# A layer with two attentions and a ternary feed-forward: the last tile's transposed context read from memory, and the maximum scans of two weights moved

## The reference

```python
x = x + cross(layernorm(x), ctx_2048)          # x: 16 x 64 x 1024, ctx_2048: 16 x 1601 x 1024
x = x + diff_attention(layernorm(x))           # causal, 8 heads, within each batch of 64 tokens
x = x + ffn(layernorm(x))

def cross(x1, c):                              # 16 batches
    energy = einsum('bcn,bmn->bcm', x1, c)     # 64 x 1601, contraction over n = 1024
    attn = softmax(energy, -1)
    attn = attn / (1e-9 + attn.sum(axis=1, keepdims=True))
    x_r = einsum('bcm,bmn->bcn', attn, c)      # contraction over m = 1601
    t = x1 - (conv_w @ x_r + conv_b)
    return x1 + relu(batchnorm(t))             # statistics over all batches

def ffn(x):                                    # W1: 4096 x 1024, W2: 1024 x 4096
    h = gelu(x @ ternarize(W1).T + b1)
    return fake_quant_4bit(h @ ternarize(W2).T + b2)

def ternarize(W):                              # needs max |W| of the whole matrix first
    delta = 0.05 * max(abs(W)); mask = abs(W) > delta
    return sum(abs(W) * mask) / max(sum(mask), 1) * sign(W) * mask
```

## Time and profile before

| | |
|---|---|
| median of three runs | 1379.93 us (1379.62 to 1380.21) |
| the profiled execution | 1379.24 us, its span 1377.4 us |
| PE busy | 1334.1 us (97%) |
| DVE busy | 878.7 us (64%) |
| ACT busy | 495.1 us (36%) |
| moved by DMA | 356.25 MB, mean 259 GB/s |

### The profile page before, as it was taken

The page is one execution under the profiler, slowest core; times in us unless marked ns, Lnnn a source line. Parts: engine busy times, 40 slices in busy tenths (PEclk is TensorE's granted clock), DMA queues, the critical chain, the costliest instruction groups (busy, mean ns, idle before and its releaser), DMA issues.

```text
span 1377.4 us, 17833 instructions
## 1 busy us (share of the span) xinstructions
PE 1334.1 (97%) x6850; PEld 651.2 (47%) x6850; DVE 878.7 (64%) x1484; ACT 495.1 (36%) x765; POOL 2.4 (0%) x10
## 2 busy tenths in 40 slices
PE   7999999999999979999999999999999999999994
PEld 4554646444454434444555555444444444444442
DVE  3232424324242288888889996755999997777974
ACT  1121302113021122116877775112545455544432
POOL 0000000000000000000000000000000000000000
PEclk9999999999999989999999999999999999999998
DMA  9999999999999587845565669341487775222264
GB/s 379 419 421 420 421 422 420 422 421 421 417 398 393 234 321 255 315 168 164 161 182 154 172 174 339 107 168 52 167 271 226 242 264 196 77 77 77 77 180 152
DMA packets 141044, 356.25 MB, mean 259 GB/s; under 512 B 63008, under 2 KB 89760, under 8 KB 115360
## 3 DMA queue, kind: packets, MB, share of 16 engines
q1 hardware_dynamic: 137792, 343.56, 68.5%
q10 hardware_dynamic: 3168, 11.54, 2.1%
HBM read 308.40 MB, written 46.66 MB: 258 GB/s over the span
## 4 chain that ended last, share of the span: by engine, by line
PE 74%; issue 14%; DMA 6%; DVE 4%; ACT 1%; DVEq 0%; POOLq 0%; POOL 0%
PE ps L1048 13%; PE ps L1153 13%; PE ps L1309 9%; PE ps L1220 8%; PE ps L962 7%; PE ps L1269 6%; PE ps L1107 5%; PE ps L1000 4%; DMA ctxT<-in_ctxT 3%; PE ps L979 2%; PE ps L1030 2%; PE ps L982 2%; DMA w_scan<-in_w2t 1%; PE ps L1173 1%; DMA x_t<-in_x 1%
## 5 line engine op out<-in xcount | busy, mean ns | idle before, releaser
L1358 PE MATMUL ps<-t_half,hl 128*128 128x512 f16 x896 | 193.6, 379 | 0.0
L1048 PE MATMUL ps<-ctx_sb,attnT 128*64 128x512 f32 (+1 forms) x832 | 180.3, 593 | 0.0
L699 ACT ACTIVATE stg<-ps 128x512 f32<-128x512 f32 (+1 forms) x80 | 44.4, 555 | 345.5 <-PE ps L979 173.4
L1358 PEld LDWEIGHTS ps<-t_half,hl 128*128 128x128 f16 x896 | 87.7, 98 | 105.7
L962 PE MATMUL ps<-ctxT,x1T 128*64 128x512 f32 x512 | 115.8, 596 | 1.8 <-DMA ctxT<-in_ctxT 1.8
L872 ACT ACTIVATE hl<-hb,al 128x512 f16<-128x512 f32 x112 | 79.2, 720 | 97.4 <-PE ps L1358 83.7
L1048 PEld LDWEIGHTS ps<-ctx_sb,attnT 128*64 128x64 f32 (+1 forms) x832 | 58.9, 137 | 115.4 <-issue 108.0
L1862 DVE SCALAR_TENSOR_TENSOR hl<-hb,al,hl 128x512 f16<-128x512 f32 x112 | 81.9, 749 | 48.7 <-ACT hl L872 48.5
L1107 PE MATMUL ps<-wv_sb,x2T 128*128 128x512 f32 x256 | 112.0, 596 | 0.0
L1220 PE MATMUL ps<-wo_sb,oT 128*128 128x512 f32 x256 | 111.6, 593 | 0.3 <-ACT oT L778 0.3
L1456 DVE COPY stg<-ps 128x512 f32<-128x512 f32 (+1 forms) x80 | 50.9, 639 | 82.2 <-PE ps L982 43.0
(11 more groups left out here) (220 smaller groups left out, 1810.5 us busy)
## 6 DMA issues: line engine op xcount, KB each, us to landing
ctxT<-in_ctxT SPq DMA_DIRECT2D x64, 1024.0 KB, 22.4
ctx_sb<-in_ctx SPq DMA_DIRECT2D x40, 1024.0 KB, 17.3
ctx_sb<-in_ctx SPq DMA_DIRECT2D x8, 4096.0 KB, 28.3
ctx_sb<-in_ctx SPq DMA_DIRECT2D x16, 2048.0 KB, 32.5
w_scan<-in_w1t SPq DMA_DIRECT2D x32, 512.0 KB, 6.4
w_buf<-in_w1t SPq DMA_DIRECT2D x32, 512.0 KB, 4.1
w_scan<-in_w2t SPq DMA_DIRECT2D x32, 512.0 KB, 5.5
w_buf<-in_w2t SPq DMA_DIRECT2D x32, 512.0 KB, 4.7
```

The lines of the kernel that those rows point to most:

```text
L1048: ins = mm(bank(ea + hf)[C * b:C * b + C, :], attnT[0:w, slots[mt], C * b:C * b + C], ctx_sb[0:w, mt, b, hf * BANK:hf * BANK + BANK], star ...
L1358: ins = mm(bank(b), hl[:, r % RING, n, s * P:s * P + P], t_half[:, r % BRING, :], start=(fresh and k == 0 and n == 0), stop=(k == HK - 1 a ...
```

## The change

Tile 7 has no transposes. The host gives two more layouts of the context: `ctxW`, the rows 1024 to 1535 transposed, and `ctxE`, the last 65 rows of tile 7 transposed. SP loads tile 7's share: two pieces of `ctxW` into the ring, two into `stg`, and two of `ctxE` into `tail0` (where `x_t` lay) and `tail1` (where tile 6's `x1T` lay). PE multiplies from there (`loaded_energies`, `tail_energies`), and the copies of ACT and DVE go. Tile 7's `load_N` stand behind these loads and in the order in which the last tile uses them. `tok` and `xo` are loaded in two parts each, the second behind `wv`; on ACT `relu(2)` stands behind tile 0's copies. Of the scans, 32 (all of W1) stand in the value projection, spread between the parts of a tile's work by `V_SCANS`, and all 32 of W2 in the output projection: four ahead of `normal(H)`, five after each tile until they are done (tiles 0 to 4, and three after tile 5).

```diff
--- before.py
+++ after.py
 SINGLES = [(mt, half) for mt in range(TM, MT) for half in range(2)]
-PAIRS = [("wide", c) for c in range(NC)] + SINGLES[-2:]
-E = len(PAIRS)
-assert len(SINGLES) == E
+LOADED = (0,) * (NT - 2) + (0, NC)
+
+
+def pairs(p):
+
+    if p < BY_ROW:
+        return SINGLES
+    return [("wide", c) for c in range(LOADED[p], NC)] + (SINGLES[-2:] if p < NT - 1 else [])
+
+
+def first_pair(p):
+
+    return sum(len(pairs(q)) for q in range(p))
+
+
+def slots_of_tile(p):
+
+    ring = [(p, "chunk", c) for c in range(NC)] + [(p, "wide", i) for i in range(min(LOADED[p] // 2, 2))]
+    return ring if p < NT - 1 else ring + [(p, "apart", i) for i in range(2)]
+
+
+USES = [use for p in range(NT) for use in slots_of_tile(p)]
+USE_NO = {use: n for n, use in enumerate(USES)}
+RING_NO = {use: n for n, use in enumerate([use for use in USES if use[1] != "apart"])}
+RING_USES = list(RING_NO)
...
-SCANS_V = 48
+SCANS_V = 32
+V_SCANS = (0, 0, 2, 5, 6, 6, 6, 6, 1)
...
+        def slot(use):
+
+            return ctxT[:, RING_NO[use] % SLOTS, :, :] if use[1] != "apart" else stg[:, 2 * use[2]:2 * use[2] + 2, :, :]
+
+        def halves(use):
+
+            return slot(use) if use[1] == "apart" else slot(use).rearrange("p c (b m) -> p c b m", b=2)
...
-            def load_T(q, chunks):
+            def load_T(q, chunks, kind="chunk"):
                 for c in chunks:
-                    k = NC * q + c
+                    use = (q, kind, c)
+                    k = RING_NO[use]
                     if k >= SLOTS:
-                        sp.wait_ge(ctxT_used, k - SLOTS + 1)
-                    sp.dma_start(ctxT[:, k % SLOTS, :, :], ctxT_in[q, c]).then_inc(ctxT_got[k % SLOTS], 16)
+                        sp.wait_ge(ctxT_used, USE_NO[RING_USES[k - SLOTS]] + 1)
+                    to, src = (slot(use), ctxT_in[q, c]) if kind == "chunk" else (halves(use), ctxW_in[q, c])
+                    sp.dma_start(to, src).then_inc(ctxT_got[k % SLOTS], 16)
+
+            def load_apart():
+
+                sp.wait_ge(e_done, first_pair(NT - 1))
+                for i in range(2):
+                    sp.dma_start(slot((NT - 1, "apart", i)), ctxW_in[NT - 1, 2 + i]).then_inc(apart_got, 16)
+                for i in range(2):
+                    sp.dma_start(tails[i][:, :, :, :], ctxE_in[i]).then_inc(apart_got, 16)
...
                     load_T(p + 1, range(7, NC))
+                    load_T(p + 1, range(min(LOADED[p + 1] // 2, 2)), "wide")
+                    if p + 1 == NT - 1:
+                        load_apart()
+                        next_N((5, 7, 0, 1, 2, 6, 3, 4))
+                        break
                     next_N(range(0, 5))
...
-            sp.wait_ge(ctxT_used, NC * NT)
+            def load_tok(t0, t1):
+                sp.dma_start(tok[:, t0:t1, :], n_dram[t0:t1].rearrange("t p n -> p t n")).then_inc(n_in, 16)
+
+            def load_xo(t0, t1, s):
+                sp.dma_start(xo[:, t0:t1, :], x_v[t0:t1].rearrange("t p n -> p t n")).then_inc(s, 16)
+
+            sp.wait_ge(ctxT_used, len(USES))
             sp.wait_ge(n_stored, 16 * (NT - 1))
-            sp.dma_start(tok[:, 0:NT - 1, :], n_dram[0:NT - 1].rearrange("t p n -> p t n")).then_inc(n_in, 16)
+            load_tok(0, 2)
             sp.wait_ge(pv_done, G * NT - 7)
-            for i in range(2):
-                h4 = slice(4 * i, 4 * i + 4)
-                sp.dma_start(xo[:, h4, :], x_v[h4].rearrange("t p n -> p t n")).then_inc(s_in[i], 16)
+            load_xo(0, 2, s_in[0])
             sp.wait_ge(pv_done, G * NT - 3)
             sp.dma_start(wv_sb[:, :, :], wv.rearrange("(c p) n -> p c n", p=P)).then_inc(wv_in, 16)
+            load_tok(2, NT - 1)
+            load_xo(2, NT, s_in[1])
             sp.wait_ge(pv_done, G * NT)
...
-                if n == 34:
+                if n == 28:
                     sp.wait_ge(xs_ready, 6)
                     load_qk(0)
...
-                if t + 2 < NT:
+                if 1 <= t < NT - 2:
...
+                if t == 0:
+                    act.wait_ge(n_in, 32)
+                    relu(2)
...
+            def loaded_energies(p):
+
+                wides = [u for u in slots_of_tile(p) if u[1] != "chunk"]
+                for j, use in enumerate(wides):
+                    if use[1] == "apart":
+                        pe.wait_ge(apart_got, 64)
+                    else:
+                        k = RING_NO[use]
+                        pe.wait_ge(ctxT_got[k % SLOTS], 16 * (k // SLOTS) + 16)
+                    for i in range(2):
+                        c = 2 * j + i
+                        for b in range(2):
+                            ins = mm(bank(2)[C * b:C * b + C, :], x1T[:, p % 2, c, C * b:C * b + C], halves(use)[:, i, b, :],
+                                     start=(c == 0), stop=(c == NC - 1))
+                    ins.then_inc(ctxT_used, 1)
+
+            def tail_energies(p):
+                for c in range(NC):
+                    for b in range(2):
+                        ins = mm(bank(3, TAIL)[C * b:C * b + C, :], x1T[:, p % 2, c, C * b:C * b + C],
+                                 tails[c // 4][:, c % 4, b, :], start=(c == 0), stop=(c == NC - 1))
+                ins.then_inc(e_done, 1)
...
                 weigh_ctx(p)
-                if p + 1 < NT:
+                if p + 1 < NT and LOADED[p + 1]:
+                    chunk_energies(p + 1, range(4, NC))
+                    if p == 5:
+                        loaded_energies(6)
+                        two(pair_transposes, 6, 0)
+                        two(pair_transposes, 6, 2)
+                        two(pair_energies, 6, 0)
+                        later_pairs(6)
+                    else:
+                        loaded_energies(7)
+                        tail_energies(7)
+                elif p + 1 < NT:
                     chunk_energies(p + 1, range(4, NC - 1))
...
-                if t % 4 == 0:
-                    V.wait_ge(s_in[t // 4], 16)
+                if t in (0, 2):
+                    V.wait_ge(s_in[t // 2], 16)
...
-                V.wait_ge(e_done, E * p + E - 2)
+                if p < NT - 1:
+                    V.wait_ge(e_done, first_pair(p + 1) - 2)
+                else:
+                    V.wait_ge(ctxT_used, used_by(p))
+                    own.done(V.tensor_reduce(mx4[:, 0:1], ps[:, ea * BANK:(ea + 2) * BANK], AX.X, ALU.max))
+                    V.wait_ge(ctxT_used, len(USES))
                 own.done(V.tensor_reduce(mx4[:, 1:2], bank(2), AX.X, ALU.max))
                 if p + 1 < NT:
                     put_x1T(p + 1)
-                V.wait_ge(e_done, E * p + E)
+                V.wait_ge(e_done, first_pair(p + 1) if p < NT - 1 else first_pair(p) + 1)
                 own.done(V.tensor_reduce(mx4[:, 2:3], bank(3, TAIL), AX.X, ALU.max))
...
+            def next_scans(n):
+                for _ in range(n):
+                    scan(scanned_tiles[0], w_scan)
+                    scanned_tiles[0] += 1
+                    if scanned_tiles[0] == WT:
+                        V.wait_ge(scanned, WT)
+                        V.tensor_reduce(wpk[:, 0:1], wmx[:, 0, :], AX.X, ALU.max).then_inc(wmax_ready, 1)
+
+            def norm2(t, scans=0):
                 if t:
                     V.wait_ge(relu_done, t + 1)
                     own.done(V.tensor_tensor(xo[:, t, :], xo[:, t, :], tok[:, t, :], ALU.add))
                 row_stats(xo[:, t, :], None if t else 0)
+                next_scans(scans)
                 V.wait_ge(root_ready, NT + 2 + t)
                 inverse_root(own, rs[:, 0, 0:1], rs[:, 1, 0:1], rs[:, 2, 0:1], t8[:, 0:1])
                 if t >= 2:
...
             both(1)
             norm2(1)
             V.tensor_reduce(al[:, 1:2], b1_sb, AX.X, ALU.max, apply_absolute_value=True).then_inc(bmax_ready, 1)
-            n_scan = 0
-            for t in range(2, NT + 1):
-                for _ in range(SCANS_V // 7 if t < NT else SCANS_V - 6 * (SCANS_V // 7)):
-                    scan(n_scan, w_scan)
-                    n_scan += 1
-                    if n_scan == WT:
-                        V.wait_ge(scanned, WT)
-                        V.tensor_reduce(wpk[:, 0:1], wmx[:, 0, :], AX.X, ALU.max).then_inc(wmax_ready, 1)
-                if t < NT:
-                    both(t)
-                    norm2(t)
+            for t in range(2, NT):
+                n = V_SCANS[t]
+                next_scans((n + 1) // 3)
+                both(t)
+                next_scans((n + 2) // 3)
+                norm2(t, n // 3)
+            next_scans(V_SCANS[NT])
...
-            for _ in range(2):
+            for _ in range(4):
                 scan(n_scan, w_scan2)
                 n_scan += 1
             normal(H)
...
-                for _ in range(3 if t else 2):
+                for _ in range(5):
                     if n_scan < 2 * WT:
                         scan(n_scan, w_scan2)
                         n_scan += 1
...
```

(2 more changed lines are left out.)

59 lines of the change are left out of this document (32 added, 27 removed).

## The result

| | before | after |
|---|---|---|
| median, first comparison | 1379.78 us (4 runs, 1377.90 to 1380.21) | 1367.33 us (4 runs, 1366.84 to 1369.86) |
| profiled execution | 1379.24 us, span 1377.4 | 1366.84 us, span 1365.0 |
| PE busy | 1334.1 us | 1322.6 us |
| moved by DMA | 356.25 MB | 360.95 MB |

The ratio is 0.9916, 95% interval 0.9899 to 0.9933. In two later comparisons of the same two kernels the ratio was 0.9913 (0.9900 to 0.9927) and 0.9914 (0.9900 to 0.9928), with medians of 1368.79 and 1368.55 for the changed one. One execution of the kernel before in the last comparison took 6973.44 us and is not in the ratios.

What follows compares the result with a forecast made beforehand. The prediction took PE's own work as the bound (1334.1 of 1377.4 us busy). Its terms, -8.70 for tile 7's transposes, 0 for the value projection and 0 for the output projection, took 1379.93 to 1371.2 us, range 1369.0 to 1374.2.

Steps and rivals of the forecast that it cites:

- Tile 7, -8.70 us: PE in tile 7: four removed blocks of 16 wide transposes at 1.89 us and one narrow at 1.14 save 8.70 us.
- The energies stay: Tile 7's energy matmuls on PE: same number and shapes, so their time was taken as unchanged.
- The clock: Rival: half-clock price of some 3.4 us behind PE's pauses changes; 1367.8 us if unpaid, 1374.6 if paid twice; chance 0.08.
- both places: Half clock at tile 7's `weights_T` after the `conv_s` pause and at the value projection's first rows, some 3.4 us together.
- The value projection, 0 + 0: Value projection: new load order and moved scans make no PE wait, so they cost and give 0.
- The slack at tile 2: Value projection: tile 2's `x2s` ready at 504.5, wanted by PE at 510.4, 5.9 us to spare.
- DVE starts the heads' sums: After the value projection: DVE begins these sums some 10 us earlier, worth nothing because PE did not wait for them.
- The loads of tile 7: 4.7 MB of transposed context land from 415 to 424 us, then tile 7's rows by about 457; cost 0.
- DMA as a giver-back: Rival: late rows or scans make PE wait 2 to 6 us in `weigh_ctx(7)` or at `x2s(2)`: 1373 to 1377; chance 0.08.
- The output projection: 16 more scans there add 18 us of DVE work, hidden beside PE's 14.61 us tile period; cost 0.
- slower: Rival: `relu(2)` blocks ACT until late `tok`, delaying tile 1's `x2s`; `tok` landing at 503 gives 1381.6 us; chance 0.03.
- nothing: Rival: idle time before `weights_T(7)` grows by what the transposes leave, so the time stays at 1380 us; chance 0.03.

Runs made afterwards that it cites:

- the spare transposes: Changed kernel plus 16 unused identity transposes between tile 7's wide energies, in one block or four blocks of 4: 1371.19 and 1372.58 us.
- spare matmuls: Changed kernel plus unused identity matmuls ahead of three PE waits (7, 4 and 16 of 128x256): 1366.18 and 1365.86 us; also added to other kernels.
- four chunks of tile 6: Changed kernel with spare matmuls ahead of three PE waits, and four of tile 6's wide context chunks also loaded already transposed: 1363.96 us, ratio 0.9883.

## Why the prediction was partly right

**Tile 7, -8.70 us.** The transposes went with their full length; `weights_T` started at 447.4 (449.0 forecast). The failed sentence is "The energies stay [...] so their time stays too": I took 7.5 us for the 32 wide records and 7.12 for the chunks' because the earlier trace rows show such blocks only beside transposes, and both took 6.87. The term was mis-sized by 0.78 us, and the spare transposes show that it is the alternation. This is a step that failed in every comparison.

**The clock.** I named this rival at 0.08 and priced it for both places together: 1367.8 if not paid. In the first profile of after one of the two was not paid, -1.50, and in the second and third, of the same kernel, both were. The forecast's error was to hold what one execution of before showed as the kernel's own, and to make the range 1369.0 to 1374.2 from it. How many executions of the first comparison escaped the first fall is not shown, but for the profiled one.
The Trainium skill, "TensorE: Matmul & The Clock Gate", Part 1, says that the gate's rhythm does not start with the kernel, so that the penalty varies from launch to launch; by that rule the trace agrees: 3.07 and 4.73 us for the same block of the same kernel.

The clock was not the whole miss. In the third profile both prices were paid as before (46.74 against 46.78 us), and its execution still took 1368.01 us, below the range: of 11.2 us of span, 9.48 are tile 7, 0.76 were there at its start, 0.52 lie in the first head, and 0.4 in the rest. The range's lower end left 2.2 us for what the energies, the wait for `kT` and the spread of one kernel's executions take together. The three executions of before known then lay within 0.6 us; in the later comparisons they ran from 1376.99 to 1382.65. The ratios of the three comparisons agree (0.9916, 0.9913, 0.9914), so the miss is not one of the first comparison's alone.

**The value projection, 0 + 0.** All steps came as worked out, mostly earlier: `wv` at 479.0 (481.5), the second part of `tok` at 485.4 (487.7), first scan's data at 497.2 (496.4), `x2s(1)` done at 489.1 (492.2) against 492.8, `x2s(2)` at 505.2 (504.5) against 507.4 us, when PE wants it. The slack at tile 2 was 2.2 us, not 5.9: PE wanted it 3.0 us earlier than I counted: 0.83 from the start of the program, 0.78 from the energies, 1.50 from the clock, less 0.18. So the forecast held for both edits together, but for the 0.52 us of the first head: "DVE starts the heads' sums some 10 us earlier, which PE did not wait for" overlooked the 0.25 us for `kT`. What I did not see is how the edits depend on each other: beside the loaded context the fuller queue asks for the new order (3.6 us), and the new order asks for the moved scans (15.1 us). The new order alone, without either, was not run. "Costs and gives 0" is right for their sum beside the old kernel and wrong as the value of either in the new one. The 3.4 us between `x2s(2)` in the earlier trace rows and its want in the earlier trace rows were all that six scans a tile leave, and a PE that comes 9 us earlier, while the first scan's data come at 499.1 instead of 494.8, uses them up. The wait for `kT`, 0.25 us before, was a sign of it.

**The loads of tile 7.** Landed at 414.5 to 423.1 (415 to 424), the rows from 437.0 to 460.1 (440 to 457), no wait. DMA as a giver-back, the rival at 0.08, did not come with the new order; with the old one it did in size (1374.35 and 1372.43, its 1373 to 1377), but at `bnm` and `wv` and not in `weigh_ctx(7)` or at `x2s(2)`.

**The output projection.** PE kept 14.61 us; five scans took 4.59 us for four and a fifth behind 0.28; DVE still waited 11.0 us for PE in total, where it was 28.5 before; `pieces` were issued up to 921.3 (932) and first used at 949.7. Cost 0, as forecast.

**The others.** The rival "slower" by `relu(2)` had 3.7 us of room at `x2s(1)` and was not seen; "nothing" is excluded. 0.8 us of the first comparison were there before tile 7 and belong to no edit.

## What to carry to other kernels

Price a removed instruction by the start-to-start time of a timeline in which its neighbours stand without it: here the alternation of transposes and energies cost the neighbours 0.78 us as well. When a stage behind the change has an engine with a few us of slack, count that slack anew for PE's earlier arrival while the data arrive when they did: edits that cost nothing together can each be what keeps the gain. And where PE idles for a few us, look for the clock behind it: read it from two executions rather than one, and try spare matmuls in the pause, but only where the stage behind has room to take the earlier start.

## What the runs showed of the hardware

- For one kernel and one and the same pause of 3.35 us, the granted clock held in one execution and fell to 1.2 GHz in another; the same rows of tile 7 stand ahead of both without a gap. It fell in 10 of 11 profiles without spare work there, and the price was 1.5 to 1.7 us on a block of 3.07. Spare matmuls over the pauses kept it up at these places in all six profiles that had them, but for a fall with four chunks of tile 6 (0.50 from 475 to 478), where the wait for `bnm` was 2.0 us in spite of them.
- A change between 128x128 transposes and 128x64 energies costs PE some 0.14 us (8.92 against 9.77 us for the same instructions over six changes more).
- The queue moved 391 GB/s from 400 to 460 us, where the earlier trace rows have 365, and 428 from 440 to 450, where they have 422. That is 1.6 MB more in the 60 us; 2.6 MB more of the new 4.7 took the place of the `tok` that is now loaded later.
- Six scans in a row through a ring of four loads, refilled only as scans end, made DVE's tile 14.6 to 17.0 us long with the new order, where six scans of 1.13 and the rest, 512.67 + 0.81 - 507.75 = 5.7, make 12.5. In the kernel before, with the same six, it was 13.9 to 15.5.
